# Expert MLP of an adaLN block: the gate product with the weights held in the array, and no turn of the activations

## What is computed

```
tidx, tw = route(x)                        # top 4 of 16 experts, per row
g = einsum('nh,eih->nei', x, w1)           # E=16 experts, I=192, H=256
u = einsum('nh,eih->nei', x, w3)
hact = silu(g) * u * combine[:, :, None]
y = einsum('nei,ehi->nh', hact, w2)
shared = (silu(x @ ws1.T) * (x @ ws3.T)) @ ws2.T
return y + shared                          # then x + gb * (...)
```

## Time and profile before

| | |
|---|---|
| median of 3 runs | 3273.53 us |
| the profiled execution | 3268.49 us, span 3266.7 us |
| mean granted clock of PE in it | 0.971 |
| first gate product of an expert job | 2239.5 us from the start of the span |
| last one | 3259.9 us |

### The profile page before, as it was taken

One profiled execution on the slowest core, in us unless ns is written; L12 is line 12 of the kernel. 1 busy time (PEld: TensorE's weight loads), 2 busy tenths in 40 slices (PEclk: granted clock), 3 DMA queues, 4 the chain that ended last, 5 costly groups with the idle time before them and its releaser, 6 DMA issues.

```text
span 3266.7 us, 57407 instructions
## 1 busy us (share of the span) xinstructions
PE 2982.8 (91%) x20658; PEld 1480.7 (45%) x20660; DVE 2246.3 (69%) x4894; ACT 1594.8 (49%) x2593; POOL 1309.1 (40%) x1685
## 2 busy tenths in 40 slices
PE   7888699999999999889899899988899989999998
PEld 4433133334433344333334333335666656666665
DVE  7887398887788887799987787712572224444487
ACT  2322456665466765466655466663333333333333
POOL 6756111224522134321136657533106653332274
PEclk9989799999999999899999999999999999999999
DMA  5842613221312231221233433234237655554486
GB/s 165 206 119 79 129 34 61 58 59 50 96 32 37 57 82 52 68 48 32 46 77 112 117 109 117 66 122 121 86 92 229 212 172 149 148 147 138 136 241 194
DMA packets 282483, 350.68 MB, mean 107 GB/s; under 512 B 61308, under 2 KB 239116, under 8 KB 281948
## 3 DMA queue, kind: packets, MB, share of 16 engines
q1 hardware_dynamic: 251324, 271.80, 30.7%
q0 software_dynamic: 30208, 71.87, 7.4%
q10 hardware_dynamic: 672, 3.34, 0.4%
HBM read 206.51 MB, written 139.21 MB: 106 GB/s over the span
## 4 chain that ended last, share of the span: by engine, by line
PE 51%; DVE 14%; ACT 12%; POOL 6%; issue 4%; DMA 2%; SPq 1%; POOLq 0%; DVEq 0%; ACTq 0%
PE PB L1094 12%; ACT P L1570 11%; DVE mx L1400 10%; PE PB L1032 8%; PE PB L1121 8%; PE PB L979 5%; PE PB L1002 4%; PE PB L1015 4%; PE PB L1044 4%; POOL yg L1753 2%; PE PB L1107 2%; PE PB L1083 2%; POOL x_slots L1740 1%; PE PB L1065 1%; POOL P L1690 1%
## 5 line engine op out<-in xcount | busy, mean ns | idle before, releaser
L1400 DVE TENSOR_REDUCE mx<-PB 128x1 f32<-128x512 f32 (+3 forms) x2560 | 1392.2, 602 | 256.2 <-PE PB L979 187.3
L1570 ACT ACTIVATE P<-PB 128x1024 f32<-128x1024 f32 (+3 forms) x1280 | 1085.6, 893 | 716.6 <-PE PB L1015 713.1
L979 PE MATMUL PB<-KO,QO 64*128 64x512 bf16 (+3 forms) x2560 | 764.4, 356 | 83.1 <-DVE mx L1400 59.2
L1032 PE MATMUL PB<-P,V 128*17 128x512 f32 (+3 forms) x5120 | 606.7, 547 | 18.5 <-POOL P L1690 18.5
L1002 PE MATMUL PB<-QO,KO 64*128 64x512 bf16 (+3 forms) x2560 | 528.4, 357 | 50.1 <-ACT P L1570 26.0
L1094 PE MATMUL PB<-W,xT 128*128 (+1 forms) x1400 | 517.7, 493 | 20.5 <-issue 20.1
L979 PEld LDWEIGHTS PB<-KO,QO 64*128 64x128 bf16 x2560 | 200.7, 94 | 715.3 <-DVE mx L1400 557.7
L1015 PE MATMUL PB<-QO,KO 34*128 34x512 bf16 (+3 forms) x2560 | 499.9, 354 | 2.2 <-DMA QO<-nh 2.1
L1690 POOL TENSOR_SCALAR_AFFINE_SELECT P<-P 128x256 f32<-128x256 f32 x512 | 204.9, 411 | 603.7 <-ACT P L1570 599.2
L1492 DVE TENSOR_TENSOR ha<-sl,PB 128x192 f32<-128x192 f32 x350 | 123.6, 353 | 428.1 <-ACT sl L1615 427.8
L1753 POOL DMA_INDIRECT yg<-y_slots,sidu x256 | 245.6, 959 | 332.2 <-DVE acc L1484 173.9
(11 more groups left out here) (169 smaller groups left out, 3191.6 us busy)
## 6 DMA issues: line engine op xcount, KB each, us to landing
xq<-x_slots SPq DMA_DIRECT2D x286, 128.0 KB, 2.4
qk_parts<-pt SPq DMA_DIRECT2D x192, 128.0 KB, 2.4
KO<-qk_parts SPq DMA_DIRECT2D x192, 128.0 KB, 5.0
y_slots<-yo SPq DMA_DIRECT2D x191, 128.0 KB, 1.7
QO<-qk_parts SPq DMA_DIRECT2D x64, 256.0 KB, 4.0
rden<-rden_rows SPq DMA_DIRECT2D x256, 64.0 KB
y_slots<-mx SPq DMA_DIRECT2D x95, 128.0 KB
v_rows<-vst SPq DMA_DIRECT2D x16, 544.0 KB, 3.5
```

The source lines that it names most:

```text
L979: mm = pe.matmul(PB[:, bank, 0:n], QO[half, k3, j, 128 * t:128 * t + 128], KO[half, k3, j, 512 * kc:512 * kc + n], start=True, stop=True)
L1032: mm = pe.matmul(PB[32 * j:32 * j + 17, 7, c0:512], V[:, g % 2, kt, 17 * j:17 * j + 17], P[:, pbuf(g, i, j // 2), j % 2, 0:n], start=kt == ...
L1400: dve.tensor_reduce(mx[:, j, t, kc:kc + 1], PB[:, u.bank[item], 0:n], AX.X, ALU.max).then_inc(s["mx"], 1)
L1570: act.activation(P[:, pbuf(g, i, p), :, 0:n], PB[:, 2 * p:2 * p + 2, 0:n], ACT.Exp, scale=0.25).then_inc(s["exp"], 1)
```

## The change

The roles of the gate's operands are exchanged: the weights become stationary, the activations moving. The product then comes out with the hidden units on the partitions, as down needs it, and the turn of `ha` falls away with its copy.

- `jw`, new, on ACT: a copy of the job's expert weights (2 x 384 columns a partition) from `W13` to `ws`, two buffers, sliced by a register that ACT loads itself, 8 numbers at once. Shared jobs take `W13`'s slice 16 directly.
- `jgate` on PE: three blocks of 128 stationary columns, each over both halves of the input, moving 128 columns. The host orders the columns as w1 (192), w3's last 64, w3's first 128.
- ACT's Silu covers 256 columns (64 of them are not used), and DVE multiplies in two instructions, 64 and 128 partitions, straight into `haT`.
- `jdown` works on 128 rows and on 64 rows filled up with zeros to 128. DVE clears `W21`'s and `haT`'s lower rows at `w2`. Down has banks 4 and 5; the units alternate between 6 and 7.
- Order in iteration m: `jdown` m-3, `jw` m, `jin` m, `jgate` m-1. PE's register load comes with `jdown`. The residual's loads (`xload`) wait for the gates of all slot jobs, since `ws` lies over `xs`.

```diff
@@ plan, run
-                elif m - n == 2:
-                    o("jturn", n)
+            if n0 <= m - 3:
+                o("jdown", m - 3)
...
+            if m < n1:
+                if jobs[m][0] == "x":
+                    o("jw", m)
+                o("jin", m)
...
+            if n0 <= m - 1 < n1:
+                o("jgate", m - 1)
@@ plan
-    u.banks = [7]
+    u.banks = [6, 7]
@@ PE, jgate
-                    for f in (0, 1):
-                        mm = pe.matmul(PB[:, 2 + k, 0:2 * I], xT[:, k, f, :], W13[f][:, expert(n), :], start=f == 0, stop=f == 1)
+                    if kind == "x":
+                        q.wait_ge(s["ws"], n + 1)
+                    for m in range(3):
+                        for f in (0, 1):
+                            w = ws[:, k, f] if kind == "x" else W13[:, f, E]
+                            mm = pe.matmul(PB[:, 2 + k, 128 * m:128 * m + 128], w[:, 128 * m:128 * m + 128], xT[:, k, f, :],
+                                           start=f == 0, stop=f == 1)
@@ PE, jdown
-                    k, bank = n % 2, y_bank[n]
-                    q.wait_ge(s["haT"], n + 1)
+                    k, bank = n % 2, 4 + n % 2
+                    q.wait_ge(s["ha"], n + 1)
...
+                    if n >= 2:
+                        q.wait_ge(s["yo"], n - 1)
@@ DVE, w2
+                elif name == "w2":
+                    q.wait_ge(s["exp"], 1280)
+                    dve.memset(W2[1][IH:128, :, :], 0.0).then_inc(s["p0"], 1)
+                    q.wait_ge(s["pv"], pv_last[15])
+                    dve.memset(haT[IH:128, :, 1, :], 0.0).then_inc(s["p0"], 1)
@@ DVE, jgate
-                        q.wait_ge(s["ht"], n - 1)
-                    dve.tensor_tensor(ha[:, k], sl[:, k], PB[:, 2 + k, I:2 * I], ALU.mult).then_inc(s["ha"], 1)
+                        q.wait_ge(s["dn"], n - 1)
+                    dve.tensor_tensor(haT[0:IH, k, 1, :], sl[0:IH, k, 128:256], PB[128 - IH:128, 2 + k, 128:256], ALU.mult)
+                    dve.tensor_tensor(haT[:, k, 0, :], sl[:, k, 0:128], PB[:, 2 + k, 256:384], ALU.mult).then_inc(s["ha"], 1)
@@ ACT
+                elif name == "jw":
+                    (n,) = at
+                    k, (kind, p, i) = n % 2, jobs[n]
+                    q.wait_ge(s["routed"], p + 1)
+                    q.wait_ge(s["l_ew"], 16 * 2 * len(W_PARTS))
+                    if n >= 2:
+                        q.wait_ge(s["gu"], n - 1)
+                    else:
+                        q.wait_ge(s["pv"], pv_last[15])
+                    if (p, i) not in of:
+                        m, half = min(RB, NI[p] + 1 - i), i // RB % 2 * RB
+                        act.load(act_regs[half:half + m], tile_e[p][:, i:i + m])
+                        for j in range(m):
+                            of[p, i + j] = act.snap(act_regs[half + j], min_val=0, max_val=E)
+                    act.activation(ws[:, k], W13[:, :, bass.ds(of[p, i], 1), :].rearrange("p f o c -> p f (o c)"), ACT.Copy).then_inc(s["ws"], 1)
@@ ACT, jgate and jturn
-                    act.activation(sl[:, k], PB[:, 2 + k, 0:I], ACT.Silu).then_inc(s["sl"], 1)
-                elif name == "jturn":
...
-                    act.activation(haT[:, k], PB[0:IH, 4 + k, 0:256].rearrange("p (f q) -> p f q", f=2), ACT.Copy).then_inc(s["haT"], 1)
+                    act.activation(sl[:, k], PB[:, 2 + k, 0:256], ACT.Silu).then_inc(s["sl"], 1)
```

More of the change, by code:

```diff
@@ L19 @@
 E, I, G = 16, 192, 4
-IH = I // 2
+IH = I - 128
 NE = E + 1
@@ L535, in program @@
         rstd = A_("rstd", [128, 2, 4], F32)
-        W13 = [nc.alloc_sbuf_tensor_at(f"W13{f}", [128, NE, 2 * I], F32, offset=at) for f, at in ((0, qo_at), (1, ko_at))]
+        assert ko_at - qo_at == 32 * 2 * I * 4 and NE <= 32
+        W13 = nc.alloc_sbuf_tensor_at("W13", [128, 2, 32, 2 * I], F32, offset=qo_at)
         w_end = NE * 2 * I * 4
@@ L542, in program @@
         A.at = qo_at + w_end
-        W2 = [A("W20", [IH, NE, 256], F32)]
+        W2 = [A("W20", [128, NE, 256], F32)]
         GB = A("GB", [128, 4, 256], F32)
@@ L686, in program @@
                 freed[item] = (s["cnt_v"], o.n(*before))
+        start = o.items.index(("experts",))
+        after = {item for item in o.items[start:] if item in u.bank}
+        read_by = {"max": "mx", "nturn": "nl", "o_proj": "xo", "o_turn": "lT", "o_logits": "L", "cnt": "cnt_v"}
+        done_before = [(s[sem], sum(item[0] == name for item in o.items[:start])) for name, sem in read_by.items()]
+        banks_free = {6: done_before, 7: [(s["oc"], 64)]}
         def max_n(g, j):
@@ L699, in t_h2 @@
             return s[f"w_h2{i % 3}"], rows_done["w_h2", i]
-        two = o.items.index(("cnt", 1, 1))
-        two = next(at[0] for name, *at in o.items[two:] if name == "jdown") + 1
-        y_bank = {n: 6 if n < two or (n - two) % 2 == 0 else 7 for n in range(len(jobs))}
-        y_free = {n: n if n <= two else n - 1 for n in range(1, len(jobs))}
         block = ctx.enter_context(nc.Block())
@@ L872, in _ @@
                         q.wait_ge(s["fin"], o.n("fin", jobs[n - XS][2]))
-                    q.wait_ge(s["pv"], pv_last[15])
+                    q.wait_ge(s["gu"], sum(NI))
                     q.wait_ge(*t_x1(i))
@@ L1038, in _ @@
                     q.wait_ge(s["on"], o.n("on", b, 3, t // 4))
-                    if u.bank[item] == 7:
-                        q.wait_ge(s["oc"], 64)
+                    if item in after:
+                        for wait in banks_free[u.bank[item]]:
+                            q.wait_ge(*wait)
                     if item in freed:
@@ L1519, in _ @@
             q = Once(act)
+            act_regs = [act.alloc_register(f"weights{j}") for j in range(2 * RB)]
+            of = {}
             q.wait_ge(s["l_mod"], 32)
```

63 lines of the change are left out of this document (19 added, 44 removed).

## The result

The changed kernel takes 3182.39 us (median of 4 runs, 3177.78 to 3193.45) beside 3272.83 us for the kernel before (3267.82 to 3276.13). The ratio is 0.974 with an interval of 0.972 to 0.976. In the experiments the pair was run side by side four more times: 0.975 (0.973 to 0.977) and 0.974 (0.972 to 0.976) on a chip as fast as the first, 0.983 (0.978 to 0.988) and 0.980 (0.977 to 0.983) on a chip whose transfer-heavy stretches are slower for both kernels.

A forecast was written before the change was run, and what follows sets the result against it. The prediction took PE to bound the expert jobs, with POOL's gathers pacing the shared ones. Savings of 7, 17, 29 and 2 us made 55, so 3218.5 us against the median 3273.5, range 3200 to 3252.

The forecast's parts named there:

- What bounds the kernel: Expert jobs: the second stage is bound by PE alone, 2.69 us a job, at its upper clock level.
- The gate: Gate on PE: 12 f32 load-and-product pairs at 0.109 us make 1.31 us a job, against 1.29 before.
- rival (a): Gate on PE: f32 loads not covered by products, pair 0.190 to 0.217 us, total 3524 to about 3635 us; chance 5%.
- The turns and down: PE, each job: the turn of `ha` goes, minus 0.22 us; down's added rows cost nothing; job 2.40 us, 0.20 saved.
- PE's registers: PE's 36 loads of expert numbers, moved ahead of down: left unchanged at 0.67 us each (bounds 0.4 and 1.0).
- ScalarE: ACT: new weight copy of 0.83 us, 1.59 us of work a job of 2.40, slack 1.7 us, so no cost.
- The first jobs: Jobs 0 to 22: 3 us from the second banks (bounds 0 and 7) and 4 us from faster jobs.
- Between the stages: Scatter of the second half before the second stage: taken as still hidden; some 6 us cost if POOL gained nothing.
- The shared stage: Last 64 jobs: POOL's gathers set 160 us whatever PE does; only jobs after the last gather gain, 2 us.
- Sum: Whole kernel: 7 first jobs, 17 jobs 22 to 142, 29 second stage, 2 shared jobs, together 55 us saved.
- The sign: Whole kernel: faster by more than 6.5 us, the smallest difference a measurement can tell, with chance 0.89.
- The range: Whole kernel's time: 3200 to 3252 us for 8 times in 10; the forecast's own range 3203 to 3238.

The follow-up runs named there:

- The run with 64 rows: The changed kernel with down's second product over its 64 real rows, without the zeros and DVE's two clearings: 3455.8 us, ratio to the kernel before 1.001.
- less of DVE: The changed kernel without DVE's product for the last 64 hidden units in the shared jobs: shared stage 182.7 us, against 186.7 in the unaltered changed kernel.
- the changed kernel of the last set: The changed kernel unaltered, run as a base on a chip of the first kind: 3185.45 us, ratio to the kernel before 0.974.
- the sums set earlier: The changed kernel with the sums of the second half spread at 2.05 instead of 2.3 a shared job: 3178.57 us, ratio to the kernel before 0.971.
- Less of POOL: The changed kernel without one of the four gathers of each tile in the second half: shared stage 177.8 us, against 186.7 in the unaltered changed kernel.

## Why the prediction was wrong

**What bounds the kernel.** Right. The second stage was PE's alone, and its job went down by what PE was relieved of.

**The gate.** The mechanism was right, and rival (a) did not come: the f32 loads run under the products, twelve in sequence, 0.112 us a pair where I took 0.109 (bounds 0.107 to 0.115; the lower one, half of 0.217, should have read 0.108). So 12 x 0.112 = 1.34 us and not 1.31, and the job is 2.42 and not 2.40; over some 225 jobs bound by PE this term was 5 us too good. The Trainium skill (TensorE: Matmul & The Clock Gate, section The mechanism, of Part 3) has it in a list that a load overlaps running products only where it goes to another row group; the text above that list also lets it run ahead into a background weight buffer. The gate's rows do not agree with the list: all 128 rows each time, and loads 0.112 us apart. The run with 64 rows does not either, since the overlap is lost just where the rows change from 128 to 64 and back.

**The turns and down.** Right: 0.22 us less, down unchanged at 0.87. The argument behind it, that rows do not lengthen a record, holds. It would have misled for 64 rows, where the record is no longer but the load ahead of it is exposed.

**PE's registers.** This step failed. I left the loads at 0.67 us each, with 0.3 as the most that could move, because "PE's sequencer is ahead of the array by a few pairs of 0.11 us". I took for a fixed price what is a difference: 0.05 us from the release of the wait ahead of the load to its start and 0.97 to 1.03 us from there to its use, less the time by which that release comes ahead of the use. Before, `ha` came 0.28 us ahead of the gate's weights, and 0.74 us showed in each load. In the changed kernel the sequencer is 1.06 us ahead of the array when the load starts, nine to ten pairs, and nothing shows: `haT` comes 1.10 us ahead. From job 60 on that is 28 loads x 0.74 = 21 us. The kernel before with nothing but the load moved shows 20 to 28. Ahead of job 60 nothing was won: PE waits 5.4 us there for nothing that the profile shows ahead of down, and waited 3.0 before ahead of the gate. Had I read the 0.48 us idle as a question (why does a load that can run ahead show at all?), the row for the turns, waiting on `ha`, would have answered it.

**ScalarE.** Right. The weight copy took 836 ns; I took 0.83 us. The estimate by the rule of the Trainium skill (ScalarE: Activation LUTs, section What ACT_TABLE_LOAD costs) was 826, and this case agrees within 2%. Half a microsecond more of it changed nothing.

```profile
L1625 ACT ACTIVATE ws<-W 128x768 f32 x128 | 107.1, 836 | 11.5 <-issue 11.5
```

**The first jobs.** The mechanism was right, the size off: the units' second bank gave some 10 us, 8 of them in waits that the profile shows; I took 3 with 7 as the end. I summed only waits of the first hundred microseconds, and left out the counts of the routing, which wait for the bank in job 38.

**Between the stages.** I took 0, and 3 us came (14.7 to 13.0, 11.1 to 9.7). The drain there has one step less now, which may be the reason; no run tests it. I looked only at what could be late.

**The shared stage.** I took 2 us gained; 2.5 to 3 were lost. What comes behind the start of the last gather did get shorter, 26.8 us from 29.3. What failed is that the gathers' 160 us would not change: their mean record went from 971 to 1000 ns, and from first to last they took 165.6 us and not 162.1. DVE's work was 4.5 us a tile, as I had it, but the tile takes 5.2. PE's waits for `haT`, in 22 places, lie inside that pace: DVE takes its work in order, and waits for a gather at one time and for a Silu at another.

**Sum.** 55 forecast, + 21 for the registers, + 11 in jobs 0 to 60 (19 us saved where the forecast's terms give 8; the bank, at 10 us and not 3, would be 7 of the 11), + 3 between the stages, - 5 for the pair, - 5 in the shared stage = 80, and the experts' stretch shows 1013.4 - 934.8 = 78.6. The median of the first result has 90. The other 11 us are not traced to any term. Scatter between runs of both kernels is of that size, of which the profiles show 13 us ahead of the experts, and side by side on a chip as fast the medians differ by 79 and 84 us. The sign was right for the reason forecast. The range failed since I let the register loads, the one cost in the rows that had no cause beside it, move by no more than half. With the 79 to 84 us of the later pairs the time would still lie below it.

## What to carry to other kernels

An idle time that the profile puts down to nothing is a term to be explained before it is kept: ask which instruction ahead of it waits, and what would run under it if it did not. When the stationary operand is exchanged for the moving one in f32, count loads: 128 x 128 weights cost about as much as 128 streamed columns (0.112 us against 0.108), so at 64 and 128 columns the loads set the pace, and at 256 and 384 the stream did (0.22 and 0.32 us). Do not mix products of 64 rows with products of 128 in f32 without a look at PE's loads; filling up with zeros may be cheaper.

## What the hardware showed that I had not expected

- Changing the rows between products from 128 to 64 and back costs more than the zeros that avoid it: 2.79 against 2.42 us a job, with PE's loads idle 0.33 us at each change. Changing from 128 to 96 and back cost nothing.
- Halving the moving columns of a load-bound gate (128 to 64) leaves the job at 2.43 us.
- A register load of 592 ns starts 0.04 to 0.05 us after the wait ahead of it is met, and its values can be used 0.97 to 1.03 us after its start. It cost PE 0.74 us where the wait was met 0.28 us ahead of the use, 0.1 to 0.2 us where it was met 1.0 us ahead, and nothing at 1.10 us.
- A gather's record on POOL is longer where DVE is busier: 947 ns at the mean with DVE busy for half of the time (second stage), 983 at 0.77 (less of DVE), 991 at 0.87 (the changed kernel of the last set), and 1028 at 0.91 (the sums set earlier, whose row this is). Less of POOL has 989 at 0.91, so it is not DVE's share alone. What ties the two was not tested.

```profile
L1772 POOL DMA_INDIRECT yg<-y_slots,sidu x128 | 131.6, 1028 | 102.5 <-DMA y_slots<-yo 63.6 <-issue 38.3 <-DVE acc L1491 0.3
```
